# Queries, keys and values taken from a bf16 one-hot product with folded tables, in a tiny language-model tower on one core

## The reference

```
nesting, segments = syntax_info(ids)                 # nesting 0..15, segment 0..7
h = concat(pos_table[s], nest_table[nesting], seg_table[segments]) @ W
h = h + attention(layernorm(h))                      # 8 heads of 16, softmax over 512 keys
h = h + experts(layernorm(h))                        # 4 experts, relu, low rank 16, gated
```

## Time and profile before

| | |
|---|---|
| three runs | 1200.89, 1201.24, 1202.33 us; median 1201.24 |
| profiled execution | 1200.39 us, its span 1198.6 us |
| busy, share of the span | PE 93%, DVE 76%, ACT 69%, POOL 49% |
| granted TensorE clock | 1.00 from 95 to 1100 us, 0.973 in the mean |
| DMA | 123.98 MB, mean 103 GB/s |

### The profile page before, as it was taken

How to read it: one execution, slowest core, us unless ns; L and a number is a source line. 1 busy time by engine, 2 the same in 40 slices (tenths; PEclk the granted TensorE clock), 3 DMA queues, 4 the chain that set the end, 5 groups by cost and what they waited for, 6 DMA issues and landing times.

```text
span 1198.6 us, 20409 instructions
## 1 busy us (share of the span) xinstructions
PE 1112.8 (93%) x6392; PEld 455.6 (38%) x6392; DVE 910.2 (76%) x2370; ACT 823.0 (69%) x1602; POOL 592.8 (49%) x588
## 2 busy tenths in 40 slices
PE   2579999999999999999999999999999999999975
PEld 1223334444344434434344444443443444433322
DVE  6288888877888788777888887778888877788322
ACT  0217777777777777777777777777777777777841
POOL 2644555456544555565445655654455555622231
PEclk9669999999999999999999999999999999999997
DMA  3534534545454345454444455444444454441111
GB/s 84 130 81 97 123 88 113 120 110 123 103 120 105 102 106 119 116 120 105 117 107 102 102 120 125 111 107 114 112 102 100 118 127 109 109 102 44 54 56 36
DMA packets 88377, 123.98 MB, mean 103 GB/s; under 512 B 17469, under 2 KB 69054, under 8 KB 82054
## 3 DMA queue, kind: packets, MB, share of 16 engines
q1 hardware_dynamic: 86720, 121.08, 43.0%
q10 hardware_dynamic: 1550, 1.59, 0.5%
HBM read 80.81 MB, written 34.95 MB: 97 GB/s over the span
## 4 chain that ended last, share of the span: by engine, by line
PE 59%; DVE 20%; issue 4%; DMA 1%; POOL 1%; ACT 0%; SPq 0%; POOLq 0%; DVEq 0%
PE pv L635 14%; PE mix L645 12%; PE sc L624 11%; DVE negmax L882 11%; PE mix L697 7%; PE mix L662 4%; PE mix L713 3%; PE mix L702 2%; PE mix L680 2%; PE mix L657 2%; DVE out_sb L961 2%; DVE rden L901 1%; PE mix L673 1%; DVE onehot L861 1%; DVE mres L892 1%
## 5 line engine op out<-in xcount | busy, mean ns | idle before, releaser
L882 DVE TENSOR_REDUCE negmax<-mix 128x1 f32<-128x512 f32 x1024 | 669.9, 680 | 173.3 <-PE mix L645 166.2
L507 ACT ACTIVATE probs<-sc 128x512 f32<-128x512 f32 x1024 | 576.8, 598 | 183.8 <-PE sc L624 179.4
L624 PE MATMUL sc<-qstk,kstk 120*128 120x512 bf16 x1024 | 366.8, 381 | 0.8 <-ACT probs L507 0.6
L645 PE MATMUL mix<-kstk,qstk 96*128 96x512 bf16 x1024 | 357.2, 392 | 10.0 <-DVE negmax L882 4.8
L635 PE MATMUL pv<-probs,vals 128*32 128x512 f32 x2048 | 274.0, 601 | 0.0
L645 PEld LDWEIGHTS mix<-kstk,qstk 96*128 96x128 bf16 x1024 | 99.7, 98 | 347.2 <-DVE negmax L882 198.1
L460 POOL TENSOR_TENSOR ctxh<-ctx_sb,rdenb 128x512 f32<-128x512 f32 x64 | 81.3, 1271 | 258.7 <-DMA rdenb<-rden_dram 258.2
L624 PEld LDWEIGHTS sc<-qstk,kstk 120*128 120x128 bf16 x1024 | 99.5, 98 | 106.1 <-issue 36.6
L697 PE MATMUL mix<-xn2T,fc1T_sb 128*128 128x512 f32 x256 | 131.9, 599 | 0.0
L416 POOL TENSOR_TENSOR hb_sb<-h_sb,obias 128x512 f32<-128x512 f32 x32 | 40.7, 1273 | 121.6 <-DVE h L907 121.6
L565 ACT ACTIVATE hid<-mix 128x512 f32<-128x512 f32 x128 | 76.8, 600 | 24.2 <-PE mix L697 24.2
(11 more groups left out here) (116 smaller groups left out, 1067.8 us busy)
## 6 DMA issues: line engine op xcount, KB each, us to landing
stack_dram<-pieces SPq DMA_DIRECT2D x192, 128.0 KB
rdenb<-rden_dram SPq DMA_DIRECT2D x64, 256.0 KB
qstk<-stack_dram SPq DMA_DIRECT2D x32, 384.0 KB, 6.6
kstk<-stack_dram SPq DMA_DIRECT2D x32, 384.0 KB, 8.7
qstk<-stack_dram SPq DMA_DIRECT2D x32, 256.0 KB, 6.9
kstk<-stack_dram SPq DMA_DIRECT2D x32, 256.0 KB, 9.3
wrow<-w_dram SPq DMA_DIRECT2D x32, 256.0 KB
out<-out_sb SPq DMA_DIRECT2D x32, 256.0 KB, 2.7
```

The costliest lines, as they stand in the source:

```text
L507: act.activation(probs[:, c % 8, i % 2], sc[:, i % RING], ACT.Exp).then_inc(s_exp, 1)
L624: pe.matmul(sc[:, i % RING, :], kstk[0:KROWS, u, h, j * P:(j + 1) * P], qstk[0:KROWS, u, h, :], start=True, stop=True).then_inc(s_score, 1)
L645: pe.matmul(max_bank(m), qstk[0:STK, u, h, j * P:(j + 1) * P], kstk[0:STK, u, h, :], start=True, stop=True).then_inc(s_mxmm, 1)
L882: dve.tensor_reduce(negmax[:, m // NT, m % NT:m % NT + 1], max_bank(m), AX.X, ALU.max, negate=True).then_inc(s_max, 1)
```

## The change

Subtracting the mean is a linear map, so `(h - mean) @ W` equals `h @ (C W)` with C the centring matrix. At setup the kernel now builds C W for q, k and v (`centre`, `qkvC`), multiplies the class tables and the position table by it, and widens the bf16 `table` from 128 to 512 columns (embedding, q, k, v), with the position parts in `posQK` and `posV`.

For each sequence:

- `xnT` and its copy, and GpSimd's `norm` (two operations), are gone.
- q and k are each one bf16 product of `onehot` (96 rows) with their part of `table`; v is four of 128 columns. They wait for `onehot` alone.
- VectorE adds the position part to q and k (`add_qk`), in slots 2 and 5.
- 1/sigma is one number a token, and q and k have tokens along the row: `rstd1` (128 x 4) is stored to DRAM (`rstd_out`) and read back spread over 128 partitions (`rstd_in`). GpSimd multiplies q and k by it (`scale`).
- ScalarE adds the bias to q and k, now from SBUF (in slots 5 and 6), and cuts the first piece as before; it copies v whole (slot 2), and GpSimd adds `posV` and multiplies by 1/sigma into `vals` (three operations).
- The places change: v moves to slot 1, `fc1_0` and `fc1_1` to slots 9 and 10, `fc1_2` and `fc1_3` to 13 and 14, slot 15 is empty.

```diff
 PRODUCTS = [
-    ("project", -2), ("xnT", 3), ("q", 3), ("low", -3), ("k", 3), ("xn2T", -2), ("out", -3), ("gates", -2),
-    ("turn_gates", -2), ("v", 3), ("fc1_0", -2), ("embed", 4), ("mT", 1), ("fc1_1", -2), ("fc1_2", -2), ("fc1_3", -2),
+    ("project", -2), ("v", 3), ("q", 3), ("low", -3), ("k", 3), ("xn2T", -2), ("out", -3), ("gates", -2),
+    ("turn_gates", -2), ("fc1_0", -2), ("fc1_1", -2), ("embed", 4), ("mT", 1), ("fc1_2", -2), ("fc1_3", -2), ("none", None),
 ]
...
+            def store_rstd(b):
+                upto(sp, s_rstd1, b)
+                upto(sp, s_rstdin, b - 1, 16)
+                sp.dma_start(rstd_dram.rearrange("(j p) -> p j", p=P), rstd1[:],
+                             allow_slow_non_contiguous=True).then_inc(s_rstdout, 16)
+
+            def load_rstd(b):
+                upto(sp, s_scaled, b - 1, 2)
+                upto(sp, s_rstdout, b, 16)
+                sp.dma_start(rstdb[:], rstd_dram.partition_broadcast(P)).then_inc(s_rstdin, 16)
...
+            def scale(b, side):
+                upto(pool, s_rstdin, b, 16)
+                upto(pool, s_raw, b, 2, side + 1)
+                pool.tensor_tensor(qk32[:, side, :], qk32[:, side, :], rstdb[:], ALU.mult).then_inc(s_scaled, 1)
...
             def qk(b, side):
-                upto(pe, s_xnT, b)
-                pe.matmul(aux("qk"[side], 1), qkvT_sb[:, side, :], xnT[:], start=True, stop=True).then_inc((s_qmm, s_kmm)[side], 1)
+                upto(pe, s_hot, b)
+                pe.matmul(aux("qk"[side], 1), table[:, 1 + side], onehot[:], start=True, stop=True).then_inc((s_qmm, s_kmm)[side], 1)
...
+            def add_qk(b, side):
+                upto(dve, (s_qmm, s_kmm)[side], b)
+                upto(dve, s_pc1, b - 1, 2, side + 1)
+                upto(dve, s_res0, b - 1, 2, side + 1)
+                dve.tensor_tensor(qk32[:, side, :], aux("qk"[side], 1), posQK[:, side, :], ALU.add).then_inc(s_raw, 1)
```

More of the change, by code:

```diff
@@ L62 @@
 ACT_WORK = [
[L63 to L66, removed]
+    (2, 1, "v", 3, 0), (4, 0, "ctx", -1, 1), (5, 1, "qk", 3, 0), (5, 2, "xn2T", -2, 0), (6, 2, "qk", 3, 1),
+    (8, 0, "gates", -2, 0), (9, 0, "gate_exp", -2, 0), (9, 1, "relu", -2, 0), (10, 1, "relu", -2, 1),
+    (12, 0, "mT", 1, 0), (12, 0, "ctx", 0, 0), (12, 1, "wT", -2, 0), (13, 1, "relu", -2, 2), (14, 1, "relu", -2, 3),
 ]
@@ L213, in tower @@
         low = sb("low", [P, S])
+        centre = hid[:, 0, 384:512]
+        qkvT_sb = hid[:, 0, 0:384].rearrange("p (i n) -> p i n", i=3)
+        qkvC = hid[:, 1, 0:384].rearrange("p (i n) -> p i n", i=3)
+        posWT = hid[:, 2, :]
+        catWT = hid[:, 3, 0:HOT]
         out_sb = sb("out_sb", [P, NT, P])
@@ L467, in _ @@
             pool.wait_ge(s_const, 3)
+            pool.wait_ge(s_pos, 3)
             work = {
-                "rstd1": lambda b, u, _: rstd(b, mv1, ve1, rstd1, s_mv1, s_ve1, s_rstd1, s_xn, 1),
-                "rstd2": lambda b, u, _: rstd(b, mv2, ve2, rstd2, s_mv2, s_ve2, s_rstd2, s_xn2, 1),
+                "rstd1": lambda b, u, _: rstd_first(b),
+                "rstd2": lambda b, u, _: rstd_second(b),
+                "scale": lambda b, u, side: scale(b, side),
+                "v": lambda b, u, _: value(b, u),
                 "residual": lambda b, u, side: residual(b, side),
@@ L497, in _ @@
             act.wait_ge(s_qb, 1)
+            act.wait_ge(s_foldmm, 1)
+            act.copy(posWT, sc[:, 0]).then_inc(s_fold, 1)
+            act.wait_ge(s_foldmm, 2)
+            act.copy(catWT, sc[:, 1, 0:HOT]).then_inc(s_fold, 1)
+            act.wait_ge(s_foldmm, 3)
+            act.mul(qkvC[:, 0], sc[:, 2, 0:P], QSCALE).then_inc(s_fold, 1)
+            act.copy(qkvC[:, 1:3], sc[:, 2, P:3 * P].rearrange("p (i n) -> p i n", i=2)).then_inc(s_fold, 1)
+            for side in range(2):
+                act.wait_ge(s_fold2mm, 2 + side)
+                act.copy(posQK[:, side, :], sc[:, 1 + side]).then_inc(s_pos, 1)
+            act.wait_ge(s_fold2mm, 4)
+            act.copy(posV[:], mix[:, 3].rearrange("p (j n) -> p j n", j=NT)).then_inc(s_pos, 1)
             act.wait_ge(s_const, 4)
@@ L607, in _ @@
             pe.matmul(pv[:, 0:P], ones_sb[:], ob_sb[:], start=False, stop=True).then_inc(s_setmm, 1)
-            pe.wait_ge(s_setcp, 4)
+            pe.wait_ge(s_fold, 4)
+            pe.matmul(sc[0:HOT, 0, 0:3 * P], catWT, qkvC.rearrange("p i n -> p (i n)"), start=True, stop=True).then_inc(s_fold2mm, 1)
+            for side in range(2):
+                pe.matmul(sc[:, 1 + side], qkvC[:, side], posWT, start=True, stop=True).then_inc(s_fold2mm, 1)
+            for j in range(NT):
+                mm = pe.matmul(mix[:, 3, j * P:(j + 1) * P], posWT[:, j * P:(j + 1) * P], qkvC[:, 2], start=True, stop=True)
+            mm.then_inc(s_fold2mm, 1)
+            pe.wait_ge(s_setcp, 5)
+            pe.wait_ge(s_pos, 3)
             pe.wait_ge(s_table, 1)
@@ L629, in values @@
                 g, half = r // 2, r % 2
+                if r == 0 and jj == 0:
+                    upto(pe, s_v, b, 2)
                 if jj == 0:
@@ L828, in _ @@
             dve.tensor_copy(id16[:], id32[:]).then_inc(s_const, 1)
+            dve.tensor_scalar(centre, id32[:], -1.0 / P, None, ALU.add).then_inc(s_centre, 1)
             dve.memset(eps_sb[:], EPS)
@@ L970, in _ @@
                 "add_pos": lambda b, u, _: add_pos(b),
+                "add_qk": lambda b, u, side: add_qk(b, side),
                 "stats1": lambda b, u, half: stats(b, h_sb, bn1, s_h, s_bn1, half),
```

142 lines of the change are left out of this document (79 added, 63 removed).

## The result

The changed kernel takes 1500.47 us in the median of four runs (1494.87 to 1502.02), beside 1201.07 for the kernel before: 1.248 times as long, 95% interval 1.245 to 1.252. 1171 was predicted, and the range ended at 1197.

What follows compares the result with a forecast made beforehand. TensorE and VectorE were taken to bound the kernel, each in parts of a step. 1200.4 - 37 - 2 - 0.8 + 11 = 1171.6, given as 1171 us; likeliest case 1155 to 1183, whole range 1144 to 1197.

Steps and rivals of the forecast that it cites:

- What else must keep up: Other engines and the 1/sigma round trip beside the step: store's wait 1.5 us, GpSimd's cover for q 0.9 us.
- the loop as the prediction drew it: Moments in slot 13, 1/sigma round trip, stacks to slot 8, back to slot 13: 26 us, cover 6.7 us.
- its own signs of being wrong: Row-max products of slot 8 wait for the stacks, exponentials wait for GpSimd, or Stretch B grows.
- The rival in which the store of 1/sigma holds up the stacks: 512 packets at 0.3 us each make the loop 34 us: no gain in the steps, 1211 us; chance 0.12.
- Stretch B: Output addition to last reduction before slot 11's value products, VectorE's, 10.4 us: VectorE's list the same, gain 0.
- Stretch C: Last reduction before slot 11's value products to next projection, TensorE's, 9.7 us: `fc1_3` leaves slot 15, gain 0.86 us.
- Stretch A: Projection in slot 0 to output product in slot 6, TensorE's, 13.0 us: cheaper products less waits, gain 0.5 us.
- The beginning: Setup and first loads: first one-hot 7 us later, stack loads 7 us more, about 3 given back; net loss 11 us.
- The sum: Gain of 1.4 us in 26.5 full steps, 37, plus 2 and 0.8, less 11 at the start: 1171 us.

Runs made afterwards that it cites:

- the repaired version: Changed kernel with 1/sigma stored as 128 runs of 16 bytes, two `rstd1` buffers, GpSimd's later pieces of k moved back and v last; 1190.39 us, ratio 0.991.
- the run with one store: The repaired version, but with the changed kernel's 4-byte store of 1/sigma, made for sequence 0 alone; 1192.66 us, one run.

## Why the prediction was wrong, by its own steps

- **What else must keep up, the round trip of 1/sigma: failed, the largest part.** The step took "a wait like that behind the denominators' store, 47.9 / 31 = 1.5" for the store's landing. It measured 9.1 on the mean (254.8 us, 28 times) and up to 10.2. The row behind the 1.5 is a store of runs of 128 bytes (`rden`, 32 f32 values a partition). With 7.6 us more the loop as the prediction drew it, 26 us, would be 33.6 against a step of 32.7, so hardly a loss. What made it 42.8 is that the loop was drawn wrong too: it goes not only by the stacks to slot 8, but on by the ids and the denominators' store, issued right behind the stack loads (6.4 to 10.4 us to land on the chain), to VectorE's reciprocal in slot 7, and from VectorE's slots by the copy of the context, which SyncE waits for, back to the store. In the kernel before, that store went out 7.6 us behind the ids (624.90, 632.55), since it waited for the context, and SyncE waited for its landing only 4.9 us in all. The prediction named no work queued behind the stacks. Of its own signs of being wrong two came plainly: row-max products waited for the stacks (129.9 us, 35.2 of them at the start), and B grew.
- **The rival in which the store of 1/sigma holds up the stacks (chance 0.12): the right place, the wrong price and mechanism.** It priced packets, 3 us for 512, or 9.6 in the bad case. The packets took 0.008 us each; the time was the landing. At its bad end it gave 1211.
- **Stretch B, gain 0: failed, the second cause.** "VectorE's list is the same" was true, its operations were not of the same length. The cover for a busier GpSimd was looked for only in ScalarE's waits. With the store out of the way this cost 3 us a step and more: B 13.5 in a step without GpSimd's new operations (of 36.2 us; the mean was 37.3), 10.3 with the pieces of k elsewhere. Here the profile had a hint that the prediction passed over: GpSimd's idle time lay where VectorE's operations on 32 columns took 0.2 us.
- **Stretch C, gain 0.86: right.** 8.9 in the changed kernel.
- **Stretch A, gain 0.5: mechanism right, size a little off.** In the repaired version the wait for v's copy was 0.73 us (0.85 predicted), that for VectorE's `add_qk` 0.3 (0.4). A is 12.7 in the repaired version and 13.1 in the changed kernel, against 13.0 before and 12.5 predicted.
- **The beginning, 11 us lost: the size failed, since the same store stands in it.** The first one-hot came at 26.15 (26.7 by the prediction), then the store is made twice ahead of the first stack loads, 8.3 and 8.8 us from its issue (30.78, 58.59) to its load (39.10, 67.42), and the first row-max product came at 83.52. Up to the output product of step 3 the loss is 74 us, where the prediction's terms come to about 8. In the repaired version that product is at 62.07, and the prediction's "near 65" holds for that.
- **The sum** holds for the repaired version in its steps, 33.00 us a step for 32.7, but not in the end: 1190 instead of 1171. It gains 34.12 - 33.00 = 1.12 a step, 28 us over the 25 steps from step 3 to step 28, and 1.6 in the two behind them, instead of 37 and 0.8. Of that the beginning takes 12.8 (output product of step 3, the gains of the first steps already in it), and eight of its steps from 3 to 28 are 0.3 to 1.3 us longer than 33.00, 6 us together, which the run with one store did not have; what made them longer stays open.

What stays open: why 512 separate 4-byte writes need 8 us to land after their packets are done. That it depends on element count or size is shown (2.2 us at 128 of 16 bytes), which of the two is not.

## What to carry to other kernels

Price a store by its issue to the wait it releases, never by its packets, and where no row shows one of its element size, take that as an unknown of 10 us and follow everything behind it on the queue once around the pipeline: the loop closes where an in-order engine waits for something issued late. When a change gives GpSimd work or shifts it in time, look at what VectorE does beside it: here its subtractions and casts on SBUF kept their 0.2 us only where GpSimd was idle or between two of its operations. A change that is good by its products can lose by the order of what stands around them: here a store in fewer, longer elements and two reordered lists made 1190 of 1500, 0.9% under the kernel before; either alone left 1310 and 1488.

## What the runs showed of the hardware

- A 2 KB store to DRAM in 512 elements of 4 bytes released the load that waits for it 8.3 to 11.7 us after its issue, with its packets done within 1.5 us where that was looked at; right behind 1.5 MB of loads SyncE waited 13.2 us for it on the mean; in 128 elements of 16 bytes it was 1.5 to 2.9 us.
- A small VectorE operation on SBUF (subtraction, cast, `wts`) of 0.2 us ended, in the steps shown, when GpSimd's running operation did, up to 1.0 us later than alone; three additions of 1.1 us in GpSimd's idle time cost 92 us over 32 sequences, at another place nothing.
- Waits cost TensorE twice: behind 8 us in which it was busy for 3.2, its clock was granted at 0.50 (1.2 instead of 2.4 GHz), and two expert matmuls took 2.07 us instead of 0.86.
